# Routed experts' product folded into the down projection of a pre-norm attention and expert layer

## What is computed

```python
logits = hidden @ gate_w                     # 8 experts, top 2 by value
h = relu(hidden @ up_w) ** 2                 # 1024 -> 2048
shared_out = h @ down_w                      # 2048 -> 1024
x_latent = hidden @ fc1_w                    # 1024 -> 512
expert_out = x_latent @ expert_w             # 512 -> 512
moe_out = expert_out * sum(routing_weights)  # one number per token
routed_out = moe_out @ fc2_w                 # 512 -> 1024
out = x + layernorm(shared_out + routed_out) * gamma + beta
```

## Time and profile before

| | us |
|---|---|
| median of 3 runs | 2251.51 (2247.93 to 2253.98) |
| the profiled execution | 2254.0 |
| its span, first to last instruction | 2252.2 |
| PE busy | 2213.2 (98%) |
| DVE busy | 1478.4 (66%) |
| ACT busy | 611.3 (27%) |
| POOL busy | 544.8 (24%) |

### The profile page before, as it was taken

How to read it: one execution, slowest core, us unless ns; L and a number is a source line. 1 busy time by engine, 2 the same in 40 slices (tenths; PEclk the granted TensorE clock), 3 DMA queues, 4 the chain that set the end, 5 groups by cost and what they waited for, 6 DMA issues and landing times.

```text
span 2252.2 us, 36558 instructions
## 1 busy us (share of the span) xinstructions
PE 2213.2 (98%) x15001; PEld 1423.5 (63%) x15001; DVE 1478.4 (66%) x1850; ACT 611.3 (27%) x950; POOL 544.8 (24%) x466
## 2 busy tenths in 40 slices
PE   6989999999999999999999999999999999999998
PEld 5756566666665444685487478468558648846853
DVE  7766468778986899775565466376466546637615
ACT  4333333444422664232022012112102201211200
POOL 2322000000002688252043023114204202311400
PEclk9999999999999999999999999999999999999999
DMA  8989378999887988879778876956967877795672
GB/s 231 201 193 198 78 159 210 249 244 231 193 202 192 308 305 287 281 241 283 206 215 231 242 229 207 305 190 201 283 199 221 238 235 229 208 304 174 198 232 94
DMA packets 511095, 502.75 MB, mean 223 GB/s; under 512 B 330832, under 2 KB 351440, under 8 KB 510928
## 3 DMA queue, kind: packets, MB, share of 16 engines
q1 hardware_dynamic: 501184, 470.00, 74.7%
q10 hardware_dynamic: 8880, 27.27, 4.2%
q0 software_dynamic: 864, 3.15, 0.4%
HBM read 351.44 MB, written 69.73 MB: 187 GB/s over the span
## 4 chain that ended last, share of the span: by engine, by line
PE 93%; issue 2%; DVE 2%; POOL 1%; DMA 1%; ACT 1%; SPq 0%; DVEq 0%; POOLq 0%; ACTq 0%
PE psum L97 66%; PE psum L2102 23%; PE psum L2049 4%; POOL arena L324 1%; DMA arena<-arena 1%; PE psum L2014 0%; SPq L286 0%; DVE arena L510 0%; PE psum L2015 0%; ACT arena L841 0%; DVE b_mx L956 0%; DVE a_stats L474 0%; DVE arena L995 0%; DVE arena L479 0%; DMA arena<-in_attn_x 0%
## 5 line engine op out<-in xcount | busy, mean ns | idle before, releaser
L97 PE MATMUL psum<-arena 128*128 128x256 f16 (+1 forms) x11592 | 1603.1, 301 | 11.8 <-DMA arena<-arena 6.8
L97 PEld LDWEIGHTS psum<-arena 128*128 128x128 f16 x11592 | 1134.0, 98 | 476.3 <-issue 17.6
L2102 PE MATMUL psum<-arena 128*128 128x512 f16 x2352 | 509.9, 379 | 0.0
L2102 PEld LDWEIGHTS psum<-arena 128*128 128x128 f16 x2352 | 230.2, 98 | 276.0
L1536 POOL TENSOR_TENSOR arena<-arena 128x256 f32<-128x256 f32 x70 | 95.3, 1362 | 436.2 <-ACT arena L1667 436.2
L841 ACT ACTIVATE arena<-psum,b_nb,consts 128x512 f32<-128x512 f32 x128 | 97.8, 773 | 198.3 <-DVE b_nb L960 198.3
L1807 DVE TENSOR_TENSOR arena<-arena 128x1536 f16<-128x1536 f32 (+1 forms) x28 | 58.8, 2100 | 115.8 <-ACT arena L1591 114.9
L1596 ACT ACTIVATE c_ystd<-c_ymv,c_epsc,consts 128x1 f32<-128x1 f32 x32 | 12.4, 387 | 410.8 <-DVE c_ymv L1829 410.8
L1523 POOL TENSOR_TENSOR arena<-arena 128x256 f32<-128x256 f32 x56 | 41.7, 745 | 283.6 <-DVE arena L1929 283.6
L1650 ACT ACTIVATE arena<-arena 128x768 f16<-128x768 f32 x56 | 47.2, 843 | 230.2 <-DVE arena L1929 230.2
L1654 ACT ACTIVATE arena<-arena 128x1024 f16<-128x1024 f32 x56 | 59.2, 1057 | 173.9 <-POOL arena L1529 173.9
(11 more groups left out here) (162 smaller groups left out, 1800.6 us busy)
## 6 DMA issues: line engine op xcount, KB each, us to landing
arena<-ws_in SPq DMA_DIRECT2D x210, 512.0 KB, 3.8
arena<-ws_out SPq DMA_DIRECT2D x196, 512.0 KB, 4.8
arena<-in_attn_x SPq DMA_DIRECT2D x64, 512.0 KB, 5.1
arena<-x SPq DMA_DIRECT2D x64, 512.0 KB, 6.6
arena<-ws_in SPq DMA_DIRECT2D x70, 256.0 KB, 3.7
x<-arena SPq DMA_DIRECT2D x32, 512.0 KB, 3.7
out<-arena SPq DMA_DIRECT2D x31, 512.0 KB, 6.3
ws_in<-arena SPq DMA_DIRECT2D x30, 512.0 KB, 4.4
```

Source lines behind the costliest of these rows:

```text
L97: last = nc.tensor.matmul(out, lhs(a, c), rhs(b, c), start=(c == 0 and n == 0), stop=(c == chunks - 1 and n == len(PRODUCTS) - 1))
L2102: mm = nc.tensor.matmul(product_banks(m)[:, u, :], rS[:, c, a, LEFT[m], u * P:(u + 1) * P], w2[slot_of(i, n)][:, cc, b, :], start=(c == 0 ...
```

## The change

The routed product is no longer a product of its own. Since (latent x routing factor) @ fused weight has the same shape as h @ down_w, the latents, multiplied by the routing factor of their token, become chunks 16 to 19 of the squared activations (pairs 8 and 9), and the fused weight becomes rows 2048 to 2559 of down_w. The seven half products of the down stage thus sum over ten pairs, five slots each, and the routed matmuls, their PSUM reads on DVE and the resident `wlat` parts go. The weights' pairs become 20; pairs 18 and 19 come from `wlat`, now f32 as ACT copies it, and are the same for the splits, sums and stores.

With it go these edits:

- Tokens stand along the free axis in the latents, so the routing factors are needed as a row in each partition. After `routing`, now behind pair 1, ACT sends the 512 factors to DRAM behind pair 3 (`send_route`) and loads them back, broadcast to 128 partitions, behind pair 5 (`load_route`). DVE multiplies pairs 8 and 9 by them.
- The parts, `own_parts` and `sum_parts`, with POOL's `sums_of`, run for ten pairs instead of eight.
- Block 0 does the 16 chunks of down, then the last four chunks tile by tile. `wlat`'s four slots (36 to 39) are split in iterations 16 and 17.
- Pairs 18 and 19 are late too: POOL forms their sums behind pair 2 of block 1, and ACT and DVE split them behind pair 4, where SP then waits to store them.
- M3 and M4 are computed half by half, and DVE finishes a tile of 128 tokens after each half.
- The scale of fc1_w now rests on sums of squares over partitions, which PE forms in attention with eight matmuls by ones.
- The transposes of the next block's rows move one slot or a few later (43 to 44, 53 and 57 to 56 and 61); part 3 of block 1's rows moves ahead of the copies of block 0's sums.

```diff
-    PER_M = CP // 2
+    PER_M = UP // 2
...
-    LATE_PAIRS, LATE_AT = 2, 2
-    PARTS_AT, STATS_AT, DIFFERENCES_AT, GAMMA_AT = (UP + 1, 13, 16, 17), 14, (13, 16), 4
-    IN_TIME = FIRST_PAIRS - LATE_PAIRS
+    LATE_PAIRS, LATE_AT = 2, (2, 4)
+    PARTS_AT, STATS_AT, DIFFERENCES_AT, GAMMA_AT = (UP + 1, 13, 16, 18), 14, (13, 16), 4
+    ROUTE_AT, ROW_AT = 1, (3, 5)
+    IN_TIME = LOADED_PAIRS - LATE_PAIRS
...
                 pool.tensor_tensor(r[:, 1], r[:, 1], r[:, 0], ALU.add).then_inc(u_two, 1)
-                if 1 <= p <= CP:
+                if p:
                     sums_of(p - 1, 1)
+                if first_turn(i - 1) and p == LATE_AT[0]:
+                    for n in late_pairs(1):
+                        pair_sums(n)
...
+        def send_route(i):
+            act.wait_ge(route_ready, i + 2)
+            with nc.allow_non_contiguous_dma(reason="a token per partition, 512 elements in all"):
+                act.dma_start(dram["route"][i].rearrange("(t p) -> p t", p=P), route[:]).then_inc(route_out, 16)
+
+        def load_route(i):
+            act.wait_ge(route_out, 16 * (i + 1))
+            act.dma_start(route_row[:], dram["route"][i].rearrange("(a n) -> a n", a=1).to_broadcast([P, TB])
+                          ).then_inc(route_in, 16)
...
-                    dve.wait_ge(rt_ready, R_TILES * i + n + 1)
-                    dve.scalar_tensor_tensor(part, bank(BANKS_R[n]), route[:, t:t + 1], part, ALU.mult, ALU.add
-                                             ).then_inc(rt_added, 1)
...
+                else:
+                    rows = r.rearrange("p (h u) n -> p h u n", u=2)
+                    dve.wait_ge(route_in, 16 * (i + 1))
+                    dve.tensor_tensor(rows, rows, route_row[:].rearrange("p (h a n) -> p h a n", h=2, a=1).to_broadcast(
+                        [P, 2, 2, HALF]), ALU.mult).then_inc(squared, 1)
+                if p == ROUTE_AT:
+                    routing(i, last)
...
+            pe.wait_ge(own_lo, UP + 2)
+            pe.wait_ge(part_lo, FIRST_SLOTS)
+            for t in D0_LAST:
+                for j in range(JU, PLAIN_TILES):
+                    for h in range(HALVES):
+                        mm = down(j, t, h)
...
+                if m in (M3, M4):
+
+                    for q in range(PER_M):
+                        weights(d_slot(m, q))
+                        mm = product(q, 0)
+                    mm.then_inc(half_ready, 1)
+                    for q in range(PER_M):
+                        product(q, 1).then_inc(slot_used, 1)
```

485 lines of the change are left out of this document (255 added, 230 removed).

## The result

The changed kernel takes 2273.22 us (median; 2268.03 to 2279.59) where the kernel before took 2249.78 in the same comparison (2246.03 to 2256.50). The ratio is 1.0096, with a 95% interval of 1.008 to 1.0113. The forecast was 2247.8, and the range ended at 2260. In the profiled executions the spans are 2271.6 and 2252.2, 19.4 us apart, and the two traces say where these lie.

The account below looks back on a forecast made before the run. The prediction took PE, busy 98% of the span, to bound the kernel. Its terms, -18.1 + 1.7 + 5.5 + 5.2 + 1.5 + 0.5, sum to -3.7 us: from the median 2251.5 to 2247.8, range 2238 to 2260.

Parts of the forecast that it names:

- Matmuls saved: Blocks 1 to 7: 84 fewer 512-column matmuls on PE's path, -18.1 us.
- Streaming: Down stages: loading 35 instead of 28 slots fits in idle DMA time, 0 us.
- The rival with 2266: Seven down stages each wait 2.6 us or more for loads, giving back the 18.1 us; 2266, chance 0.08.
- Latents' parts in blocks 2 to 7: Down stages of blocks 2 to 7: parts are ready 4.5 us in, so no wait, 0 us.
- Tail: After the last matmul: changed additions and statistics and a later residual load, +0.5 us (0 to 1).
- Matmuls by ones: Attention: eight more 512-column matmuls where PE has no idle time, +1.7 us.
- Block 1, down stage: Block 1's down stage: SP's loads stop for part 0 of the rows and PE may wait, +1.5 us (0 to 5).
- Block 1, up stage: Block 1: POOL's eight sums and late splits delay DVE; PE waits ahead of pairs 5 and 7, +5.2 us (0 to 11).
- End of block 0: Block 0's end: PE waits for four more slots that DVE and ACT split late, +5.5 us (2.9 to 9).
- slower: Rival, block 1: POOL and DVE exclude each other throughout, waits pass 16.4 us; +9, 2260.5, chance 0.15.
- the cover holds: Rival, blocks 0 and 1: POOL fits between DVE's instructions, few waits remain; -12.5 us, 2239, chance 0.32.
- the stream doesn't keep up: Rival, down stages: saved time was covering loads, so each of seven waits for its ring; 2266, chance 0.08.

Follow-up runs that it names:

- e3_sums: Changed kernel, but POOL takes the eight sums of pairs 18 and 19 at the end of block 0; ratio to the kernel before 1.0065.
- e2_roots: Changed kernel, but at block 0's end ScalarE takes each tile's square root one copy after that tile's copies; ratio to the kernel before 1.0053.
- e6_before_table: Kernel before, with only the staging table changed so that raw pair 13 is requested behind pair 10, not pair 8; ratio to the kernel before 1.0023.
- e5_contiguous: Changed kernel, but block 0's routing factors go to DRAM as 16 contiguous bytes a partition, giving tokens another's factor; ratio to the kernel before 1.0091.
- e11_nine: Changed kernel with early pair-13 request, moved POOL sums and square roots, contiguous factor transfer and further reordering edits; 2249.03 us, ratio to the kernel before 0.9993.

## Why the prediction was wrong, step by step

- **Matmuls saved, -18.1: right.** The down stage has 420 matmuls in 90.65 us, and the period is 184.35.
- **Streaming, 0: right.** No gap in the six last down stages. The rival with 2266 came nearest to the measured time, by a mechanism that isn't there.
- **Latents' parts in blocks 2 to 7, 0: right.** The up stage is 91.72 there, the down stage has no gap behind it.
- **Tail, +0.5: right,** +0.3.
- **Matmuls by ones, +1.7: not shown.** The scatter ahead of block 0 is larger.
- **Block 1, down stage, +1.5: right,** one wait of 1.61 for ws_out.
- **Block 1, up stage, +5.2: the mechanism right, its size partly by luck, one wait missing.** POOL's eight sums put 20.0 us between the additions of pairs 2 and 3, where the working gave 44.0 - 24.6 = 19.4. The splits behind pair 4 put 13.2 there, as forecast. PE's waits for VectorE stand ahead of pairs 5 and 7, as forecast, and are 3.58 and 0.90, 4.5 for 5.2; e3_sums removed them. What failed is the step "DVE will come free earlier, since eight reads of routed results go". It came free 18.5 us into the block instead. The first addition had been at 27.3 us for pair 2; it is now at 991.03 - 957.58 = 33.5, not at 24.6. The reads are gone, but the row norms, which had been spread between them, came in one piece behind the last copy. The wait of 5.60 comes from there: ScalarE's copy of the gate's logits stands behind the fourth square root. The working had no such wait, and e2_roots removed it. The additions' 8.9 us of lateness didn't add to the two forecast waits because PE was late too, by the 5.60 and the clock behind it. Where that wait is gone, in e2_roots, pair 2 is added 27.9 us into the block, 3.3 later than worked out, and the wait ahead of pair 5 is 6.12, near the 2.6 + 3.3 = 5.9 that the working then gives.
- **End of block 0, +5.5: the step that failed most.** Block 0 measured +25.5. The working priced what VectorE has to do (the two new pairs of splits, the multiplication), and took its shift as +1.5, with VectorE being "busy without a pause" as the reason. In the changed kernel it isn't: it stands idle for what is ahead of it. The request of pair 13 was moved by two pairs in a table that the working never costed: 7.26 us of VectorE, and 5 us of time by itself in the kernel before (e6_before_table). The routing factors' way to DRAM was costed at nothing and held a raw pair back: 4.39 us of VectorE (e5_contiguous). The working had the last split end at 914.3 + 5.5 = 919.8, 178.0 us into S; it ends at 931.88, 195.2 in, 17.2 later. These two stalls are 11.65 of it. The rest is not shown one by one; what stands in the trace is the 2.95 at the fourth pair (0.56 before), a wait of 2.69 for the load of x (0.47 before), and the low parts of the two latent pairs (2.31 and 2.32 us, where the working took 1.2 each).
- **Not in the sum at all: the clock.** 29.3 us of waits brought 13.2 us of slower matmuls with them. The forecast 12.2 us of waits would have brought some 5, by the same share. The share is no constant: gaps of 0.90 and 1.61 us brought nothing, one of 2.08 brought 1.7.

The rival that came true in sign was "slower", at 2260.5 with a chance of 0.15. Its mechanism, POOL's sums and VectorE excluding each other, is real. It is worth the 4.5 us that were in the forecast anyway, and 3.6 more in the clock and behind (e3_sums). It is not what decided, though its condition, waits of over 16.4 us together, was met. The two others, that the cover holds and that the stream doesn't keep up, are both wrong. A rule of the Trainium skill (SBUF — State Buffer, section Who interferes with whom) says that such a sum and a split hold the shared ports for the whole instruction in turn. In the 8.91 us in which VectorE made its four splits, POOL made about four sums of 2.2. Taken strictly in turn, four of 1.28 and four of 1.27 would need 10.2, so the trace agrees with the rule only in kind, as the forecast took it.

What stays open: e11_nine still has an S 11.9 us longer than the kernel before: 10.0 of waits and some 4 of slower matmuls, less the 2.6 by which block 1 is now shorter. Not tried were to copy the gate's logits ahead of the last square root, for which PE still waits 5.24, and to take the routing out of the way of the raw pair's request (3.01 at the fourth pair). Nor was it tried whether VectorE's added work in block 0 (four more splits) could be hidden at all.
